# Reading the routing gates back from DRAM: one read per pair of experts instead of two

## The reference, cut to what matters

```python
x = x + attention(layernorm_over_channels(x))            # per image, 256 tokens, 16-wide q and k
t = tokens(x)                                            # 1024 x 64
xt = layernorm(t)
logits = xt @ Wr + br                                    # 1024 x 8
top_p, top_idx = top_k(softmax(logits), 2)
weights = top_p / top_p.sum(-1)
xe = layernorm(xt) * ln_g[e] + ln_b[e]                   # for every expert e
h = gelu(xe @ W1[e] + b1[e])                             # 64 -> 256
y = h @ W2[e] + b2[e]                                    # 256 -> 64
out = t + sum over the two chosen experts of weights * y
```

## Time and profile before

| | us |
|---|---|
| median of 3 runs | 62.23 (62.0 to 62.38) |
| the profiled execution, its device time | 62.09 |
| the profiled execution, first to last instruction (span) | 60.2 |

### The profile page before, as it was taken

The page is one execution under the profiler, slowest core; times in us unless marked ns, Lnnn a source line. Parts: engine busy times, 40 slices in busy tenths (PEclk is TensorE's granted clock), DMA queues, the critical chain, the costliest instruction groups (busy, mean ns, idle before and its releaser), DMA issues.

```text
span 60.2 us, 1140 instructions
## 1 busy us (share of the span) xinstructions
PE 54.2 (90%) x332; PEld 31.2 (52%) x332; DVE 33.5 (56%) x154; ACT 33.7 (56%) x78; POOL 24.7 (41%) x48
## 2 busy tenths in 40 slices
PE   1998999799969999999999997999999999599830
PEld 0323667585847586872551674284462762232720
DVE  2279679458898959833900004799870000953920
ACT  5401568996996477959297179518749396000000
POOL 5157493000463399407329500299526000049400
PEclk9999999999999999999999999999999999999997
DMA  0451549760000000000000165510000037662011
GB/s 0 110 97 25 132 112 327 261 255 0 5 0 0 0 5 11 0 0 0 0 0 11 46 211 200 210 45 1 0 0 0 11 110 203 210 171 91 0 44 44
DMA packets 4309, 4.43 MB, mean 74 GB/s; under 512 B 2188, under 2 KB 2896, under 8 KB 4304
## 3 DMA queue, kind: packets, MB, share of 16 engines
q1 hardware_dynamic: 3984, 4.34, 24.0%
q10 hardware_dynamic: 320, 0.03, 0.5%
HBM read 4.08 MB, written 0.29 MB: 73 GB/s over the span
## 4 chain that ended last, share of the span: by engine, by line
PE 78%; DVE 8%; issue 3%; DMA 3%; ACT 1%; POOL 1%; ACTq 0%; POOLq 0%
PE banks L892 27%; PE banks L917 25%; PE banks L848 7%; PE banks L821 4%; PE banks L802 4%; DMA X<-in_x_dram 3%; PE banks L786 3%; PE banks L870 2%; PE banks L810 2%; DVE gated L662 1%; PE banks L861 1%; POOL rs L287 1%; PE banks L955 1%; PE banks L933 1%; DVE X L508 1%
## 5 line engine op out<-in xcount | busy, mean ns | idle before, releaser
L428 ACT ACTIVATE H<-banks,PF 128x512 f32<-128x512 f32 x32 | 20.0, 683 | 9.3 <-PE banks L892 9.3
L892 PE MATMUL banks<-XE,W1F 64*128 64x256 f32 x128 | 16.8, 395 | 0.0
L917 PE MATMUL banks<-H,W2F 128*64 128x512 f32 x64 | 15.3, 602 | 1.0 <-issue 1.0
L892 PEld LDWEIGHTS banks<-XE,W1F 64*128 64x128 f32 x128 | 11.6, 186 | 6.2 <-issue 5.2
L323 POOL TENSOR_TENSOR acc<-acc,gated 128x512 f32<-128x512 f32 (+1 forms) x6 | 6.5, 1089 | 14.3 <-DVE gated L662 14.1
L309 POOL TENSOR_SCALAR XE<-XF,PF,LB 128x256 f32<-128x256 f32 x15 | 8.3, 564 | 4.1 <-ACT XF L409 4.1
L662 DVE SCALAR_TENSOR_TENSOR acc<-banks,B2T,GS 128x512 f32<-128x512 f32 x2 | 1.5, 751 | 12.8 <-DMA GS<-gates_kept 12.8
L917 PEld LDWEIGHTS banks<-H,W2F 128*64 128x64 f32 x64 | 4.3, 136 | 8.4 <-issue 8.3
L293 POOL TENSOR_TENSOR rs<-base,half 128x4 f32<-128x4 f32 x4 | 4.1, 1028 | 9.6 <-DVE base L571 9.6
L786 PE MATMUL banks<-zeros 128*128 128x512 f16 x17 | 6.4, 497 | 1.3 <-POOL zeros L326 1.3
L662 DVE SCALAR_TENSOR_TENSOR gated<-banks,B2T,GS 128x512 f32<-128x512 f32 (+1 forms) x7 | 4.6, 670 | 2.3 <-PE banks L917 1.6
(11 more groups left out here) (81 smaller groups left out, 62.0 us busy)
## 6 DMA issues: line engine op xcount, KB each, us to landing
GS<-gates_kept SPq DMA_DIRECT2D x16, 128.0 KB, 2.9
W1F<-in_w_dram SPq DMA_DIRECT2D x1, 768.0 KB, 4.9
W2F<-in_w_dram SPq DMA_DIRECT2D x1, 512.0 KB, 4.7
W1F<-in_w_dram SPq DMA_DIRECT2D x1, 256.0 KB, 3.2
out_dram<-res SPq DMA_DIRECT2D x4, 64.0 KB, 2.0
X<-in_x_dram SPq DMA_DIRECT2D x2, 64.0 KB, 1.9
X<-in_x_dram SPq DMA_DIRECT2D x1, 128.0 KB, 2.6
WQK<-in_attn_w_dram ACTq DMA_DIRECT2D x2, 16.0 KB, 2.3
```

The lines of the kernel that those rows point to most:

```text
L428: nc.scalar.activation(H[:, r, :].rearrange("p (t n) -> p t n", t=PT), ps_z[g // J % 2][:, :, PIX * j:PIX * j + PIX], ACT.Gelu, bias=PF[:, ...
L892: nc.tensor.matmul(ps_z[q % 2][:, k, PIX * j:PIX * j + PIX], W1F[rows, e, j, :], XE[h][rows, e, :], start=True, stop=True).then_inc(z_read ...
L917: mm = nc.tensor.matmul(ps_y[s % 2][C * k:C * k + C, :], W2F[:, u, :], H[:, (2 * J * s + J * k + j) % RING, :], start=(j == 0), stop=(j == ...
```

## The change

The two reads of a pair, each of one expert's row over 64 partitions, are replaced by one read of both rows over 128 partitions. On the DRAM side its access pattern is 2 experts x 64 repetitions x 512 tokens; on the SBUF side it is the whole tile, 128 partitions x 512. The wait in `weigh` counts 16 instead of 32. The bytes that arrive and where they arrive are the same.

```diff
                     sp.wait_ge(gates_out[h], 16)
-                for k in range(2):
-                    sp.dma_start(GS[s][C * k:C * k + C, :], gates_kept[h, 2 * p + k, :].partition_broadcast(C))\
-                        .then_inc(gates_in[s], 16)
+                sp.dma_start(GS[s][:, :], gates_kept[h, 2 * p:2 * p + 2, :].unsqueeze(1).broadcast_to([2, C, TOK]))\
+                    .then_inc(gates_in[s], 16)
...
                 dve.wait_ge(y_ps, 2 * (s + 1))
-                dve.wait_ge(gates_in[s], 32)
+                dve.wait_ge(gates_in[s], 16)
```

## The result

The changed kernel takes 91.05 us, median of 4 runs (90.84 to 91.19), against 62.16 us (62.0 to 62.38): a ratio of 1.464, 95% interval 1.458 to 1.469. The prediction was 88.7 us, from 84.8 to 95. The profiled execution took 91.1 us, with a span of 88.8. Times are medians over all runs of a kernel, and a ratio compares its undisturbed runs with those of the kernel before that were measured beside it, so that where the two differ, the ratio times 62.2 us is the better figure.

A forecast was written before the change was run, and what follows sets the result against it. The prediction took PE to bound the kernel, with gates arriving only just in time. Last pair at 82.4 plus 4.5 gave a span of 86.9, plus 1.9 around it 88.8, written as 88.7 us; range 84.8 to 95.

The forecast's parts named there:

- to weigh(0): Half 0, first read's issue to pair 0's gates: 1.9 us fixed plus 5.6 us of rows, landing at 40.3.
- two reads, to weigh(2): Half 0, after pair 0: one pair every 5.6 us, so weigh(2) waits until 51.5 instead of starting at 40.00.
- weigh(2) to the write of half 1: Between the halves: 4.1 us of routing, gates ready at 55.6, then some 0.65 us; write issued at 56.25.
- write to first read: Half 1, on SP: it goes on 1.91 us after the write, at 58.15.
- three reads, to weigh(7): Half 1, reads behind its first: 5.6 us each, with the last pair landing at 82.4.
- weigh(7) to the end: End of the kernel: the present 4.46 us from weigh(7) to the end of the span still comes behind it.
- Two engines: Merged gate reads: the DRAM side's leading count of 2 gives two engines, 64 rows of 2 KB each; chance 87%.
- The row: Merged gate reads: a 2 KB row costs 87 ns per engine, 64 rows 5.6 us; range from 81 to 96 ns.
- The fixed time: Around a read's rows: 1.9 us, bounded by 1.7 and 2.5, counted once for each half.
- The wait between the halves: From half 1's gates to their write: transpose 0.28, copy 0.26, with the steps between some 0.65 us.
- The clock: TensorE may fall to 1.2 GHz in idle gaps, 0.9 us more on the path; nothing in the sum.
- Rival 1: Merged gate reads keep all 16 engines; 0.6 us less, 61.5 us; chance 10%.

The follow-up runs named there:

- the series of L: Kernel before, two reads per pair kept, DRAM side's 64 repetitions written as L x (64 / L); ratios 1.50, 1.18, 1.04, 1.00 for 2, 4, 8, 16.
- L = 8: Kernel before, two reads per pair kept, DRAM side's 64 repetitions written as 8 x 8; 65.27 us, ratio 1.036.
- copies_one: Kernel before with each expert's row written to DRAM 8 times and one read per pair; 64.88 us; its control, with two reads per pair, 64.96 us.
- L = 2: Kernel before, two reads per pair kept, DRAM side's 64 repetitions written as 2 x 32; 92.99 us, ratio 1.496.
- L = 4: Kernel before, two reads per pair kept, DRAM side's 64 repetitions written as 4 x 16; 73.19 us, ratio 1.176.

## Why the prediction was right

The spans, 86.9 forecast and 88.8 measured, term by term (measured from the rows above). Another 0.4 us lies outside the span, 2.3 us around it in the profiled execution where 1.9 was reckoned.

| term | forecast | measured | difference |
|---|---|---|---|
| first read issued, half 0 | 32.85 | 33.55 | +0.7 |
| to weigh(0) | 7.5 | 7.75 | +0.3 |
| two reads, to weigh(2) | 11.1 | 10.43 | -0.7 |
| weigh(2) to the write of half 1 | 4.75 | 7.00 | +2.25 |
| write to first read | 1.91 | 1.92 | 0 |
| to weigh(4) | 7.5 | 7.63 | +0.1 |
| three reads, to weigh(7) | 16.7 | 15.61 | -1.1 |
| weigh(7) to the end | 4.5 | 4.91 | +0.4 |

The terms that came out longer sum to 3.8 us and 0.4 outside the span, those that came out shorter to 1.8. So the mechanism was right, and that the total is as near as 2.4 us is in part luck.

- **Two engines:** right, by the completion packets, by the busy share of 2.06 engines, and by the series of L, in which nothing but the leading count changes. It was inferred from a single transfer of the kernel before, the write, whose leading counts are unequal.
- **The row:** 81 ns and not 87, at the low end that the range allowed. Both prices behind the forecast came from stretches with up to 16 engines at work, and the 87 ns were scaled down from larger rows, with small packets among them: of the 229 packets of the earlier trace rows 119 are under 512 B, and the other 110 carry 0.47 MB, some 4 KB each. Steps of 5.2 us in place of 5.57 are 1.8 us less over the five reads behind a first one, 2.5 if the two first reads had run at that pace too.
- **The fixed time:** a first read takes 2.5 us more than 64 rows at the later pace (7.63 or 7.75 less 5.2), where the prediction had 1.9. Not all of that is fixed. The DMA view of 34:40 of the changed kernel has the rows begin near 34.85, 1.3 us after the issue as before, and holds 113 of them:

```profile
DMA  0000030000011111111111111111111111111201
...
DMA packets 113, 0.23 MB, mean 39 GB/s; under 512 B 0, under 2 KB 0, under 8 KB 113
```

  That is 56 or 57 rows on each engine in 5.15 us, where 81 ns a row would allow 63 or 64. So about 0.5 us of the 2.5 are rows below their pace, and the fixed part is about 2.0, near the forecast (an estimate from these counts, for half 0 alone).
- **The wait between the halves:** the one step that was wrong in kind, "From there the transpose (0.28) and the copy (0.26) lead to SP; with the steps between them some 0.65 us". I had carried DVE's order through and not ACT's: the tanh waits for the routing, the gelus wait behind the tanh, layer1(12) and (13) behind the gelus, and turn_gates(1) behind layer1. In the kernel before the tanh waited 0.2 us for its input, and nothing was held up. Now it cost 2.45 us (3.29 less the 0.84 of the kernel with the tanh moved). The term of 7.00 us in the table is 3.90 of routing, 0.2 less than the 4.1 forecast, and 3.10 from its end to the write.
- **The clock:** the prediction left it out of the sum and allowed 1 us. It cost 1.1 us of that wait, by the run with the added matmuls, since layer1(12) and (13) stood on the path, which the prediction had not seen. At the end it cost 0.45 us. That is read from rows alone: the two groups of fold matmuls there (L946 and L954) took 1.12 and 1.06 us at a granted clock of 0.50, 1.2 GHz, and the same two took 0.66 us each in the kernel before.
- **The start:** 0.7 us before the first gate, in matmuls that both programs share: three matmuls on zeros near the start took 1.37 us in place of 0.81. The traced executions of two of the other kernels (L = 8, and the merged reads in half 0 alone) show the same, the others not; it is no part of the change, and what decides it is open.
- **Rival 1** (16 engines, 0.6 us less) is out by the 2 completion packets, and its gain is not there either: copies_one, which is that rival built, gains nothing measurable over its control.

## What to carry to other kernels

Before two transfers are made one, write down both access patterns and look at the outermost counts: a DRAM side that begins with a 2 kept 14 of 16 engines out of it, while a repeated count that can be written with 16 ahead cost nothing. The number of small completion packets of a transfer in the profile says how many engines it had. And where a step is made later, follow the order of every engine past it: an instruction that waits for nothing today (here a tanh of 0.2 us) can hold up the work behind it once its input is late.

## What was not expected

- SP stopped at an issue. Of the four merged reads of a half the first two were issued in 0.5 us each; then an issue took up to 5.06 us, and the four took 9.27 us, though SP waits for nothing there. With L = 2 the eight reads took 13.35 us, with L = 4 they took 4.51, half a microsecond each. It came with many rows outstanding per engine (128 or more, where L = 4 has that many in all); that this is the cause is not shown. The steps between the weighs stayed at 5.2 us, so the reads lost nothing by it. The write of half 0's result stood behind it (70.11, 5.54 us for two issues), off the chain that ended last.
- A read on two engines ran below its pace at first: between 35 and 40 the changed kernel moved 46 GB/s, behind that some 50; with L = 2 it was more pronounced (the 1.2 us above).
